# Sixteen-head window attention on Trainium2: attention products computed turned, with the softmax division moved to the exponentials and the second half of each tile run one tile later

## The reference, cut to what matters

```python
for i in range(DEPTH):                      # DEPTH = 6, HEADS = 16, DIM_HEAD = 64, WINDOW = 32
    x = attn_layer(shift_tokens(x), Wqkv[i], q_scale[i], k_scale[i], Wo[i]) + x
    x = ffn_layer(shift_tokens(x), ln_g[i], ln_b[i], W1[i], b1[i], W2[i], b2[i]) + x
...
# in local_attention: every window of 32 queries sees its own 32 keys and the 32 before it
sim = jnp.einsum('bhwie,bhwje->bhwij', bq, bk2) * QK_SCALE
sim = jnp.where(mask, -jnp.finfo(sim.dtype).max, sim)
attn = jax.nn.softmax(sim, -1)
out = jnp.einsum('bhwij,bhwje->bhwie', attn, bv2)
```

## Time and profile before

| | us |
|---|---|
| three runs | 2193.18, 2192.55, 2189.56 |
| median | 2192.55 |
| span of the profiled execution, first to last instruction | 2182.5 |
| its own time, if it is that of the median run: what lies around the span | 10.05 |
| tile stage, slots 0 to 95 | about 561 to 2132 |
| busy in the span: PE / DVE / ACT / POOL | 2005.7 / 1809.4 / 1579.9 / 1167.3 |

### The profile page before, as it was taken

How to read it: one execution, slowest core, us unless ns; L and a number is a source line. 1 busy time by engine, 2 the same in 40 slices (tenths; PEclk the granted TensorE clock), 3 DMA queues, 4 the chain that set the end, 5 groups by cost and what they waited for, 6 DMA issues and landing times.

```text
span 2182.5 us, 82607 instructions
## 1 busy us (share of the span) xinstructions
PE 2005.7 (92%) x34395; PEld 1457.7 (67%) x34395; DVE 1809.4 (83%) x3751; ACT 1579.9 (72%) x3031; POOL 1167.3 (53%) x1413
## 2 busy tenths in 40 slices
PE   6888899987699999999999999999999999999997
PEld 4666654455577776777777777777767777677775
DVE  7888765678798998888988888988888988888884
ACT  4777753365577887787877788777787878887773
POOL 1112110000577676666776667666667767667761
PEclk9999999998899999999999999999999999999999
DMA  4000001000122232222322223322232322332221
GB/s 114 1 2 2 2 31 59 30 1 30 52 72 68 61 105 69 68 63 71 90 72 75 66 58 95 81 68 66 70 87 71 87 58 58 102 82 62 75 59 40
DMA packets 98196, 132.18 MB, mean 61 GB/s; under 512 B 27900, under 2 KB 42882, under 8 KB 97826
## 3 DMA queue, kind: packets, MB, share of 16 engines
q1 hardware_dynamic: 97826, 126.90, 22.0%
HBM read 28.20 MB, written 1.11 MB: 13 GB/s over the span
## 4 chain that ended last, share of the span: by engine, by line
PE 72%; DVE 13%; issue 6%; ACT 6%; POOL 1%; SPq 1%; DMA 0%; DVEq 0%; POOLq 0%; ACTq 0%
PE oo L586 21%; PE pj L586 19%; PE tr L589 14%; PE sc L586 13%; ACT arena L1924 3%; PE tr L586 2%; DVE arena L1729 2%; DVE xn L1318 2%; DVE arena L1486 1%; PE oo L589 1%; DVE arena L1731 1%; DVE arena L1750 1%; DVE arena L1752 1%; PE sc L589 1%; ACT sc L1924 1%
## 5 line engine op out<-in xcount | busy, mean ns | idle before, releaser
L2345 POOL TENSOR_TENSOR arena<-arena 128x1024 f32<-128x1024 f32 x192 | 456.9, 2380 | 336.9 <-DVE arena L1731 336.9
L1924 ACT ACTIVATE arena<-tr 128x512 f32<-128x512 f32 (+2 forms) x874 | 460.8, 570 | 111.9 <-PE tr L589 109.7
L1924 ACT ACTIVATE arena<-pj 128x512 f32<-128x512 f32 x576 | 341.7, 599 | 189.5 <-PE pj L586 150.4
L589 PE MATMUL tr<-ident,arena 128*128 128x128 f32 x2882 | 413.3, 279 | 25.3 <-DMA beta<-in_L_attn_betas 9.8
L1924 ACT ACTIVATE arena<-arena 128x16 f32<-128x16 f32 (+6 forms) x808 | 362.3, 454 | 98.7 <-DVE arena L1486 74.0
L589 PEld LDWEIGHTS tr<-ident,arena 128*128 128x128 f32 x2882 | 330.6, 141 | 93.4 <-issue 34.5
L2363 POOL TENSOR_TENSOR arena<-arena 128x1024 f32<-128x1024 f32 x192 | 366.7, 1910 | 23.2 <-POOL arena L2356 0.9
L1729 DVE TENSOR_TENSOR arena<-pj,rtab 128x512 f32<-128x512 f32 x384 | 259.8, 677 | 24.8 <-ACT arena L1924 23.4
L586 PE MATMUL oo<-slab,arena 64*32 64x64 f32 (+1 forms) x12416 | 232.1, 228 | 41.0 <-issue 26.4
L1731 DVE TENSOR_TENSOR arena<-pj,rtab 128x512 f32<-128x512 f32 x384 | 261.4, 681 | 0.0
L1737 DVE TENSOR_REDUCE arena<-arena 128x8 f32<-128x512 f32 x384 | 255.6, 677 | 0.0
(11 more groups left out here) (289 smaller groups left out, 3802.5 us busy)
## 6 DMA issues: line engine op xcount, KB each, us to landing
slab<-arena SPq DMA_DIRECT2D x576, 128.0 KB, 2.4
slab<-arena SPq DMA_DIRECT2D x336, 64.0 KB, 2.0
wqkv<-in_L_ffn_Wqkv SPq DMA_DIRECT2D x18, 512.0 KB, 4.2
arena<-gate_mem SPq DMA_DIRECT2D x24, 256.0 KB, 4.3
wo<-in_L_ffn_Wo SPq DMA_DIRECT2D x6, 512.0 KB, 4.2
w<-in_L_ffn_W SPq DMA_DIRECT2D x6, 341.0 KB
YT<-in_L_attn_x SPq DMA_DIRECT2D x4, 256.0 KB, 3.5
arena<-in_L_ffn_W SPq DMA_DIRECT2D x1, 1024.0 KB
```

The lines of the kernel that those rows point to most:

```text
L589: return nc.tensor.transpose(o, i, ident[0:i.shape[0], 0:i.shape[0]])
L1924: return nc.scalar.activation(o, i, f, **k)
L2345: p_.tensor_tensor(r_, r_, rb[:, k, :], ALU.add).then_inc(sum_ok, 1)
```

## The change

Values become the weights (64 x 64) and the turned exponentials (32 columns a window) go through, so that the product comes out turned, and `turn_out`, `take_out` from `tr`, `weighted` and `On` are gone. The exponentials have two buffers; POOL divides them (`normalise`) before they are turned. All that follows the sums works on tile g-3 in place of g-2, and the layer norm, `Wo` and feed-forward pieces come one slot later: `norm_back` and `ln_apply` in t = 0, `ff_up` and `wo_half` 0 in t = 1, `ff_down` in t = 2, `wo_half` 1 and `norm_in` in t = 3. `shifted` and `low_half` of 384 columns stay in t = 0. On ACT `take_out` now stands between `copy_v` 0 and `inverse_root` 0. `windows` and SP's order are as before, but for `wo_weights` (four DMAs, in t = 3) and `ff_weights` (in t = 2). `lcur`, a copy of one layer's columns of `lcol`, is gone.

```diff
 PE
-            def turn_out(g, j): ... 4 transposes of On into tr, on_tr
             def turn_probs(g, j):
+                pe.wait_ge(en_ok, g + 1)
                 for u in range(4):
                     pr = 4 * j + u
-                    last = tp(tr[:, j, u * P:(u + 1) * P], Ex[:, 2 * pr:2 * pr + 2, :])
+                    last = tp(tr[:, j, u * P:(u + 1) * P], Ex[g % 2][:, 2 * pr:2 * pr + 2, :])
-            def values(n, g, t, i):
-                wait(pe, on_ok, g)
-                for pr in range(4 * i, 4 * i + 4):
-                    for u in range(2):
-                        for w in range(G):
-                            last = mm(oo[q, u, pr * DL:(pr + 1) * DL], PT[d, pr, q],
-                                      V2[d, t % 2, w, pr * DL:(pr + 1) * DL], skip_group_check=True)
+            def values(g, i):
+                    wait(pe, o_cp, g * 2)
+                for a_ in (2 * i, 2 * i + 1):
+                    for w in range(G):
+                        for pr in (2 * a_, 2 * a_ + 1):
+                            for u in range(2):
+                                d, c = slice(u * DL, (u + 1) * DL), (u + pr) % 2
+                                last = mm(oo[c * DL:(c + 1) * DL, u, a_ * P + w * WIN:a_ * P + (w + 1) * WIN],
+                                          V2[d, t % 2, w, pr * DL:(pr + 1) * DL], PT[d, pr, q],
+                                          skip_group_check=True)
...
-                if t == 2 and m1 is not None:
+                if t == 3 and m1 is not None:
                     pe.wait_ge(xs_f, m1 + 1)
-                    pe.wait_ge(on_ok, min(g - 1, NTILE))
+                    pe.wait_ge(o_cp, (g - 2) * 2)
                     norm_in(LNB, LNB_BANKS[0], xsF)
 DVE
-            def soft2(g):
+            def sums(g):
                 ve.wait_ge(e_exp, g + 1)
-                v.tensor_reduce(sm, Ex, AX.X, ALU.add).then_inc(sm_ok, 1)
+                wait(ve, en_ok, g)
+                v.tensor_reduce(sm, Ex[g % 2], AX.X, ALU.add).then_inc(sm_ok, 1)
-            def weighted(g): ... On <- oo * ri, 128 x 1024
 ACT, slot
                 copy_v(g, t, 0)
                 if layer_end:
                     weights_high(l + 1, 1)
+                if g >= 3:
+                    take_out(g - 3, 0)
+                    take_out(g - 3, 1)
+                if t == 0 and m2 is not None:
+                    norm_end_(m2, LNB_BANKS[1])
                 inverse_root(g, 0)
 POOL
+            def normalise(g):
+                gp.wait_ge(ri_ok, g + 1)
+                p_.tensor_tensor(e_, e_, ri.unsqueeze(2).broadcast_to([P, HL, 2 * WIN]), ALU.mult).then_inc(en_ok, 1)
             def slot(s_):
                 add_parts(g, t, 0)
+                if g >= 2:
+                    normalise(g - 2)
                 add_parts(g, t, 1)
                 newton(g, 0)
                 if t == 0:
                     low_half(n * 2 + 2, YT[:, s_.y0:s_.y0 + S], P, S)
                 scaled(g, t, 0)
 drain: a third tile, TX = NTILE - 3; on PE both ff_up of MY and last_down(MY) ahead of norm_in
+                ff_up(MY, 1, LAST_FF[MY][1])
+                pe.wait_ge(ff_ev, MY * FFC + 1)
+                ff_up(MY, 2, LAST_FF[MY][2])
                 pe.wait_ge(o_cp, NTILE * 2)
                 last_out_project(1)
...
+                last_down(MY)
                 pe.wait_ge(xs_f, MZ + 1)
-                norm_in(LNB, LAST_NORM[0], xsF)
-                last_down(MY)
+                norm_in(LNB, oo[:, 0], xsF)
```

More of the change, by code:

```diff
@@ L402, in __init__ @@
                 self.g = self.n * T + t
-                first, last = l == 0, l == DEPTH
-                self.later = 0 < l < DEPTH
-                self.new = not last
-                self.c_ = t < 1 and b == 0 if last else not (first and b == 0 and t < 1)
-                self.d_ = t < 2 and b == 0 if last else not (first and b == 0 and t < 2)
-                self.m1 = None if (first and b < 1) or (last and b > 0) else self.n - 1
-                self.m2 = None if first and b < 2 else self.n - 2
-                self.l1 = l if b >= 1 else l - 1
-                self.l2 = l if b >= 2 else l - 1
-                self.y0, self.y1, self.y2 = ((b - k) % B * S for k in range(3))
-                self.ahead = None if last or (b == B - 1 and l == DEPTH - 1) else (b + 1) % B * S
+                self.later = l > 0
+                self.m1 = self.n - 1 if self.n >= 1 else None
+                self.m2 = self.n - 2 if self.n >= 2 else None
+                self.y0, self.y1 = b * S, (b - 1) % B * S
+                self.ahead = None if b == B - 1 and l == DEPTH - 1 else (b + 1) % B * S
         def run_slots(slot):
@@ L1232, in last_out_project @@
                 for p_ in range(PAIRS):
[L1233 removed]
+                    last = mm(WOB[i][:, half], wo[:, p_, :], oT[:, p_, half], start=(p_ == 0),
                               stop=(p_ == PAIRS - 1))
@@ L1256, in drain @@
-                values(NB - 1, TA, T - 2, 0)
+                    turn_probs(TX, j)
+                pe.wait_ge(lnb_norm, MY + 1)
+                values(TX, 0)
+                for j in range(2):
+                    pe.wait_ge(pt_cp, TX * 2 + j + 1)
+                    turn(TZ, T - 1, 2 + j)
+                values(TX, 1)
+                pe.wait_ge(qk_cp, TZ * 4 + 3)
+                norm_back(LNB, LNB_BANKS[1], MY)
+                window_scores(TZ, T - 1, 0)
+                window_scores(TZ, T - 1, 1)
@@ L1257, in drain @@
+                pe.wait_ge(lnb_out, MY + 1)
+                for j in range(2):
+                    turn_probs(TA, j)
+                pe.wait_ge(v_cp, TZ * 2 + 2)
+                ff_up(MY, 0, LAST_FF[MY][0])
+                values(TA, 0)
+                values(TA, 1)
+                pe.wait_ge(t_sub, TZ + 1)
+                pe.wait_ge(o_cp, TA * 2)
+                last_out_project(0)
+                final(0)
                 for j in range(2):
                     pe.wait_ge(pt_cp, TA * 2 + j + 1)
-                    turn(TZ, T - 1, 2 + j)
@@ L1844, in slot @@
-                if d_:
-                    weighted(g - 2)
-                if new and b == B - 1 and t == 0 and l < DEPTH - 1:
-                    tables(l + 1)
-                if new:
-                    lengths(g, 3)
-                    clamp(g, 1)
-                    crossing(g, 4)
-                if t == 0 and m2 is not None:
+                m1, m2 = s_.m1, s_.m2
+                if b == 0 and t == 0:
+                    weights_low(l, 1)
+                    ve.wait_ge(tab_ok, l * 2 + 1)
@@ new lines, in slot @@
+                wait(ve, qk_tr, (g - 2) * 4 + 2)
+                rotate(g, t, 0)
+                rotate(g, t, 1)
+                lengths(g, 0)
+                crossing(g, 1)
+                if t == 1 and m2 is not None:
+                    ff_gate(m2, 0, FFB[0])
+                if t == 0 and m2 is not None:
+                    ln_apply(LNB, LNB_BANKS[0], m2)
+                if g == 0:
+                    crossing(g, 2)
+                lengths(g, 1)
+                if g > 0:
+                    crossing(g, 2)
@@ new lines, in slot @@
+                if t == 1 and m1 is not None:
+                    add_attention(m1, 0)
+                if t == 2 and m2 is not None:
+                    add_ff(m2, oo[:, 0])
+                if t == 3 and m1 is not None:
+                    add_attention(m1, 1)
+                if g >= 2:
+                    sums(g - 2)
+                if b == 0 and t == 0:
+                    ve.wait_ge(tab_ok, l * 2 + 2)
+                wait(ve, qk_tr, (g - 2) * 4 + 4)
+                rotate(g, t, 2)
```

542 lines of the change are left out of this document (215 added, 327 removed).

## The result

| | median us | runs | to the kernel before |
|---|---|---|---|
| before | 2191.14 | 2189.56 to 2193.18 | 1 |
| after | 2440.01 | 2437.31 to 2442.20 | 1.1131 (95%: 1.1115 to 1.1146) |

The change makes the kernel 249 us slower. The forecast was +115 us, 2307.5, with a range of 2225 to 2350: the sign was right, but the size forecast is less than half of the one measured, and the time lies outside the range. The span of the profiled execution is 2439.1 us, and the mean granted clock of TensorE is 0.944.

The account below looks back on a forecast made before the run. PE was taken to bound three of four slots, a DVE chain the fourth (t = 3). Batches +64, key weights +49 and ends +2 gave +115 on 2192.55: 2307.5 us, range 2225 to 2350.

Parts of the forecast that it names:

- `xs_lo` hand-off: From new t = 0 to 1, projection 0 waits for POOL's low half behind `take_out` and `ln_finish`: 3.65 us a batch.
- key weights: At five layer ends they queue behind late `windows` DMAs, holding ACT and `norm_in`: stall 9.8 us each, +49.
- `norm_in` behind `take_out`: In new t = 3, `norm_in` waits for `take_out` behind `copy_v` 0 instead of `weighted`: +1.22 us a batch.
- products turned: On PE, 64 loads of 64 columns take 0.88 us a half against 0.70: +0.18 a half, +0.36 a tile.
- turning removed: Eight PE transposes of `turn_out` go: -1.02 us in each of new t = 1, 2, 3; nothing in t = 0.
- `normalise`: POOL's added 1.91 us product fits a gap between two `add_parts`, its result wanted one slot later: costs nothing.
- ends: Drain: `last_down` ahead of `norm_in`, +3 us; first slots lose a tile's work, -1; sum +2.
- faster: Rival: both hand-offs and `norm_in` are covered, each of 96 slots gains 0.66 us; 2132 us, chance 0.12.
- weights in time: Rival: at layer ends the DMA queue does not hold ACT; 2259 us, chance 0.12.
- xs_lo hidden: Rival: POOL is ahead in t = 0 to 1, only the layer-end weights stall; 2227 us, chance 0.06.
- loads two at a time: Rival: in the products, only two PE loads overlap, 1.76 us a half, +2.12 a tile; 2466 us, chance 0.06.
- Not ahead: Rival: POOL's division is not done ahead of its turn, PE waits 1.91 us a tile; +183, 2490 us, chance 0.02.

Follow-up runs that it names:

- three edits: On the changed kernel: low half before `newton` 0, key weights issued before `windows`, first half of products waiting for the first copy alone; together 2269.39 us, ratio 1.0359.
- last three experiments: On the drain-edited kernel, `normalise` last in t = 0: 1.0101; on top, separately, rotation 0 between `soft1`'s steps: 1.0184, or t = 0 low half on DVE: 1.0137.
- e1_low_first: On the changed kernel, POOL does `low_half` of 384 columns ahead of `newton` 0 in slots t = 0; 2353.47 us, ratio 1.0745.

## Why the prediction was wrong in size

| term of the sum | forecast us | what the runs showed |
|---|---|---|
| `xs_lo` hand-off | 3.65 x 22 = 80 | 85 by undoing most of it, and 18 more with the low half earlier still |
| key weights | 49 | 54 by undoing it; 45 when put into the kernel before |
| first half's wait for both copies | not in it | 50 by undoing it, 47 when put into the kernel before |
| `norm_in` behind `take_out` | 1.22 x 22 = 27 | 29 |
| products turned | +0.18 a half | +0.28 a half |
| turning removed | -1.02 in three slots of four | gone; of the three, only t = 2 became shorter (slot 58: 15.10 us, against 15.40 for slot 57 before, which did the same work) |
| `normalise` | 0 | 0 in t = 0; 168 where it is late |
| ends | 2 | drain +16.8; 10 back by order |

**The step that failed** is that the sum left a wait out. For the steps that are moved I had costed DMAs, copies and queues, but in `values` I read the loops and not the number in the semaphore: `pt_cp` for the first half went from g * 2 + 1 to g * 2 + 2. Two experiments from opposite sides give 47 and 50 us for it, the largest part of the 134 us that the forecast lacked. Next come the `xs_lo` hand-off with up to 23 over its 80 (85 + 18), the products' 19 and the drain's 15 (both below), and the key weights with 5. The parts overlap (three edits gave 189 apart and 169 together), and some 20 us stay with no step of their own. Most of them may be `weights_low` at the layer ends, which I had put at nothing: in the changed kernel weight loads of PE waited 17.8 us in five for it, in the kernel before none is shown waiting. No run isolates it.

**Mis-sized terms.** *Products:* the estimate of 0.88 us a half was low; the loads alone show 1.02 and the half 1.14. The extra 0.10 in each of 192 halves is 19 us. The price of a load was right, 55 ns where the starts show 58, and so was the mechanism, four quarters side by side; the bound of 1.76 us did not come. What was wrong is the comparison: 0.88 is 64 starts of 13.8 ns without the last load's own length, and the 0.70 it was set against has that length in it (the last load of a half starts at 0.59 in the kernel before, and its record lasts 0.105). With the 137 ns of the last load's record the same estimate gives 1.0 us, and +0.3 a half. The Trainium skill's rule ("TensorE: Matmul & The Clock Gate", The mechanism), that a load overlaps a running matmul only where the row group differs, is not borne out: neighbours in the same rows but other columns left a half at 1.14 us, and only loads into the same quarter cost more, 2.47. *The ends:* I priced only `last_down` ahead of `norm_in`. On DVE `sums` of the last tile stood behind the copy of the first output, and so behind PE's last `Wo` half and turning; and all of it ran at a granted clock of 0.83, where the old drain had 0.94.

**The right number for a partly wrong reason.** The `xs_lo` hand-off was priced as a wait of 3.65 us, and the waits are 3.4 on average (58.0 in 17). But undoing it left waits of 1.1 us and gave 85 us all the same: 50 of idle time and 42 of busy time in the two profiles, because with the long wait gone the slot behind it ran at full clock. That 80 was forecast and 85 came of this one edit is luck. I priced idle time only by its length. That the same instructions take longer behind it is the part I didn't see. It shows behind the long stalls of t = 1 and of the layer ends, as busy time that is merely larger, part of it in slots that have no wait of their own. PE's busy time in the tile stage is 1522.13 in the changed kernel and 1480.83 with the three edits, 41 us less for the same work.

**What held.** The direction; the place of each of the three stalls that I named (t = 1, the layer's last slot, `norm_in`); that `wk_hi` would not follow `copy_v` at once (ACT waited 8.99 us for it); the rivals *faster*, *weights in time*, *xs_lo hidden* and *loads two at a time* are out. That `take_out`'s wait in the other slots stays hidden was right: PE shows no wait for `scaled` in the changed kernel. *Not ahead*, priced at 183, came true only where `normalise` was put last in every slot, and cost 168.

**Why nothing was gained when the stalls were gone.** The kernel with `normalise` last in t = 0 has a tile stage of 1597.50 us with PE busy for 1472.44; before it was 1571.10 and 1483.65. The change does take work off PE, but 11 us, not the 98 of the turnings: the products take some 54 back (0.28 x 192), some 10 are the projections' and `Wo`'s same records at a granted clock of 0.99 and not 1.00, and some 20 I can't assign to a row. Against that stand 38 us more of idle time. In the kernel before, the slot without feed-forward work on PE was the one that a chain on DVE bound anyway; now it is t = 0, which wants POOL's low half, sum and scaling and ACT's copies in the 12 us that PE needs (slot 56 of this kernel is 13.90 us long, with PE busy for 12.13). The last three experiments moved one step of that slot each; one changed nothing, and in two the wait went to the next engine. Whether another distribution over four slots wins was not tried.

The 26 us that are left do not lie in every batch. Three batches in a row, slots 56 to 59, 60 to 63 (the last of a layer) and 64 to 67, in the kernel before:
```profile
1474.40:1540.60 66.20, 62.85 (x1286) 47.40 (x1284) 56.27 (x95) 51.44 (x96) 44.42 (x55) 1.00 0.24 63
1540.60:1606.70 66.10, 62.66 (x1287) 47.45 (x1284) 59.53 (x102) 53.48 (x97) 46.84 (x53) 1.00 0.34 87
1606.70:1672.80 66.10, 63.02 (x1284) 47.28 (x1283) 57.04 (x96) 52.84 (x99) 45.52 (x54) 1.00 0.28 73
```
and in the kernel with `normalise` last in t = 0:
```profile
1489.70:1555.60 65.90, 61.99 (x1253) 47.02 (x1251) 51.00 (x90) 51.30 (x94) 51.86 (x59) 1.00 0.25 64
1555.60:1624.80 69.20, 63.66 (x1261) 47.99 (x1251) 55.31 (x96) 53.48 (x98) 55.45 (x60) 0.98 0.31 81
1624.80:1693.00 68.20, 63.39 (x1260) 48.16 (x1251) 53.33 (x92) 52.85 (x97) 53.45 (x59) 0.97 0.26 68
```
Inside a layer the two kernels are even; on both sides of a layer's end the new one is 3.1 and 2.1 us longer, at a lower granted clock. Over all 24 batches, by the starts of projection 0, 20 of the 26 us lie in the first and the last batch of the layers. None of the last three experiments touched what those batches do more, the loading and splitting of the next layer's weights.

## What to carry to other kernels

When a producer's consumer is moved by a stage, compare every semaphore value of the moved function, not only what it waits for: a count one higher cost about as much here as the five late loads of weights. Price a stall of some microseconds on TensorE with the work behind it at a lower granted clock, and look for that price in busy time, too, also in slots that show no wait. Compare two estimated rates only when both count the tail, or neither. When three engines are full in one slot, reordering one of them hands the wait on; look for a slot with room before moving the step.

## What the runs showed of the hardware

- Where PE had stood 3.4 to 3.5 us, its granted clock was 0.88 and 0.92 over the slot that followed, part of it at the lower of its two levels (1.2 GHz), where `ff_up` 0 took 3.51 us. With the low half first (`e1_low_first`) 22 of these 23 slots had 1.00, behind waits up to 1.8 us, and one, behind 2.1 us, 0.92. With all three edits the 13 such slots behind waits of 1.7 to 2.1 us had 0.92 in nine cases and 1.00 in four: the length of that one wait does not settle it. At a layer's end, behind 11 us, the granted clock was 0.50 over the next 5.1 us (1766.60 to 1771.70), and the matmuls of 512 columns there took 0.63 us and not 0.40.
- f32 loads of 64 columns into the four quarters of the array go in rounds of four, a round every 58 ns; into one quarter in a row they start 55 to 59 ns apart. With eight loads to a quarter before the next one a half took 2.47 us, about 39 ns a load, as the loads of two quarters overlap where the order changes. Sharing rows with the neighbour costs nothing (1.14 us either way).
- A load of 64 columns shows 137 ns in the records, one of 32 shows 105, one of 85 shows 153 and one of 128 shows 190. The durations themselves are not the rate of loads, but their difference per column, 0.86 ns, gave 55 ns for 64 columns, near the 58 between starts.
- `weights_low` of the keys on DVE, 128 x 1024, took 2.97 us in slot 64; its five runs in the changed kernel have a median of 2.96, its six in the kernel before one of 2.06, from 1.21 to 2.91. I had bounded it by the 1.23 of an operation of that size. The trace shows what the rest is. Wherever a POOL operation on 128 x 1024 was under way when a `weights_low` began on DVE (four times in the kernel before, nine in the changed one, keys and values), the DVE record ended 1.08 us behind POOL's, whatever its start. With no such POOL operation it took 1.21 or 1.22. In two cases the two began within 0.24 us of each other and POOL's was the late one, with 2.74 and 2.99 us in place of 1.91, and DVE's took 1.21. So one of the two engines stood until the other was done. With `normalise` on POOL the values' `weights_low` meets this too: 1.84 us in all five, 1.21 before.
